# GpSimd waits for each slot's gathers to land before it begins the next slot's, in both layers of a two-layer graph network

## The reference

```python
h = relu(layernorm(x)); h0 = h @ W + b
agg = segment_sum(edge_weight[:, None] * h0[src], dst, 6250)
x = x + relu(agg / (segment_sum(edge_weight, dst, 6250)[:, None] + 1e-6))
h = relu(layernorm(x))
messages = gelu(concat([h[src], edge_attr]) @ W_msg + b_msg)
x = x + gelu(((1 + eps) * h + segment_sum(messages, dst, 6250)) @ W_upd + b_upd)
```

## Time and profile before

| | us |
|---|---|
| timed runs, median of 3 | 2670.86 |
| timed runs, lowest and highest | 2669.74, 2680.39 |
| profiled execution, span | 4082.0 |

### The profile page before, as it was taken

The page is one execution under the profiler, slowest core; times in us unless marked ns, Lnnn a source line. Parts: engine busy times, 40 slices in busy tenths (PEclk is TensorE's granted clock), DMA queues, the critical chain, the costliest instruction groups (busy, mean ns, idle before and its releaser), DMA issues.

```text
span 4082.0 us, 72599 instructions
## 1 busy us (share of the span) xinstructions
PE 2950.6 (72%) x22325; PEld 2600.4 (64%) x22326; DVE 2089.7 (51%) x4376; ACT 1607.4 (39%) x5144; POOL 1835.1 (45%) x1911
## 2 busy tenths in 40 slices
PE   2776766665665666576788788778878878878887
PEld 2666665554554555565677677677767767767777
DVE  8444445544544554544455455555545545555554
ACT  2343333433433443334344444444434444444443
POOL 2333344334434434424455545545545554554552
PEclk9888787877777777787888888888888888888888
DMA  4000000000000000002333333333333333333332
GB/s 92 14 12 14 13 16 16 13 13 15 14 12 15 15 13 14 15 14 66 75 84 85 81 81 84 87 79 83 88 76 86 83 81 81 84 87 78 85 88 52
DMA packets 473123, 214.39 MB, mean 53 GB/s; under 512 B 264996, under 2 KB 442024, under 8 KB 473076
## 3 DMA queue, kind: packets, MB, share of 16 engines
q1 hardware_dynamic: 412404, 151.55, 14.2%
q0 software_dynamic: 60672, 62.25, 9.2%
HBM read 208.14 MB, written 5.51 MB: 52 GB/s over the span
## 4 chain that ended last, share of the span: by engine, by line
PE 41%; issue 11%; another core or an unknown queue 1%; DVE 1%; DVEq 0%; ACT 0%; ACTq 0%
PE ps L918 28%; PE ps L1123 6%; PE ps L988 5%; PE ps L1112 2%; DVE sel L1451 0%; PE ps L1070 0%; DVE rows L1455 0%; DVEq L1464 0%; PE ps L1017 0%; ACT eT L844 0%; DVE sums_sb L1472 0%; DVE parts L1219 0%; DVE room L1654 0%; ACT dw L652 0%
## 5 line engine op out<-in xcount | busy, mean ns | idle before, releaser
L629 POOL DMA_INDIRECT rows<-p_table,idx x1176 | 1109.4, 943 | 1065.6 <-ACT idx L660 736.0
L918 PE MATMUL ps<-parts,pick_all 128*128 128x448 f32 x5488 | 1241.0, 379 | 63.5 <-issue 59.9
L629 POOL DMA_INDIRECT rows<-h_table,idx x720 | 709.5, 985 | 1062.1 <-ACT room L760 857.7
L918 PEld LDWEIGHTS ps<-parts,pick_all 128*128 128x128 f32 x5488 | 1046.3, 195 | 193.6 <-issue 109.4
L947 PE MATMUL ps<-adj,h_sb 128*64 128x160 f32 (+1 forms) x4802 | 503.4, 342 | 516.4 <-issue 469.9
L947 PEld LDWEIGHTS ps<-adj,h_sb 128*64 128x64 f32 x4802 | 404.4, 170 | 608.8 <-issue 551.9
L1451 DVE TENSOR_TENSOR sel<-ps,mask 128x896 f32<-128x896 f32 x196 | 213.5, 1089 | 761.4 <-remote 541.9
L1388 DVE TENSOR_SCALAR hot_p<-iota_p,scal 128x256 fp32r<-128x256 f32 (+1 forms) x848 | 309.4, 365 | 410.9 <-PE ps L928 321.6
L928 PE MATMUL ps<-hot_c,hot_p 128*128 128x125 f32 (+1 forms) x2336 | 456.3, 302 | 87.6 <-issue 72.4
L721 ACT COPY adj<-ps 128x500 f32<-128x500 f32 (+1 forms) x848 | 389.8, 524 | 203.0 <-PE ps L928 126.5
L928 PEld LDWEIGHTS ps<-hot_c,hot_p 128*128 128x128 f32 x2336 | 377.4, 207 | 110.5 <-issue 86.5
(11 more groups left out here) (181 smaller groups left out, 2975.9 us busy)
## 6 DMA issues: line engine op xcount, KB each, us to landing
src_all<-keys SPq DMA_DIRECT2D x196, 448.0 KB
ea<-in_edge_attr_dram SPq DMA_DIRECT2D x196, 256.0 KB
rows<-p_table,idx POOLq DMA_INDIRECT x1176
rows<-h_table,idx POOLq DMA_INDIRECT x720
x_sb<-in_x_dram SPq DMA_DIRECT2D x6, 224.0 KB, 3.5
h_table<-h_sb SPq DMA_DIRECT2D x6, 224.0 KB
p_table<-h_sb SPq DMA_DIRECT2D x6, 224.0 KB
out_dram<-h_sb SPq DMA_DIRECT2D x6, 224.0 KB
```

The source lines that it names most:

```text
L629: nc.gpsimd.indirect_dma_start(out=rows[:, s, j, 0:D], out_offset=None, in_=table[:, :], in_offset=bass.IndirectOffsetOnAxis(ap=idx[:, s, ...
L918: last = nc.tensor.matmul(to, hot[:, k, t * P:(t + 1) * P], parts[:, part, k, :, :].rearrange("p a d -> p (a d)"), start=(k == 0 and part ...
```

## The change

`gathers` gets a third argument, the level of the slot's semaphore at which this turn's gathers have all landed. After it has issued a slot's gathers, POOL waits for that level and only then goes on to the next slot. The last body of layer 1 is called without it. `s_passed` is a counter that nobody waits for. Nothing else changes.

```diff
-                def gathers(turn, tiles):
+                def gathers(turn, tiles, landed=None):
                     for s in range(SLOTS):
                         pool.wait_ge(s_const, CONSTS)
                         pool.wait_ge(s_idx[s], turn)
...
                         for j in tiles:
                             nc.gpsimd.indirect_dma_start(
...
                             ).then_inc(s_gat[s], 16)
+                        if landed is not None:
+                            pool.wait_ge(s_gat[s], landed)
+                            pool.sem_inc(s_passed, 1)
 
                 if layer == 0:
                     for z in ZONES:
                         with pool.Fori(z.first + 1, z.end + 1) as turn:
-                            gathers(turn, range(z.JA, J))
+                            gathers(turn, range(z.JA, J), z.gathered(turn - 1) * 16 + 16 * z.JH)
                 else:
                     with pool.Fori(BODIES + 1, 2 * BODIES) as turn:
-                        gathers(turn, range(J0))
+                        gathers(turn, range(J0), 16 * GATHERED + (turn - BODIES) * (16 * J0))
                     gathers(2 * BODIES, range(J0))
```

## The result

The changed kernel takes 3438.98 us (median of 4 runs, 3428.53 to 3445.61), the kernel before 2675.62 beside it: a ratio of 1.286, 95% interval 1.282 to 1.290. That is +763 us, where +600 were forecast; the time lies 9 us above the top of the range.

What follows compares the result with a forecast made beforehand. POOL's gather issue was taken as the bound, at its limit in layer 0 and nearly so in layer 1; bodies of 22.2, 27.2 and 37.8 us with start, transition and end summed to 3266, said as 3270 us (+22%), range 3076 to 3410.

Steps and rivals of the forecast that it cites:

- The page's 45% of POOL: Whole kernel: POOL is busy for 45% of the profiled span, which taken alone says a wait on it costs nothing.
- +1.8 us in layer 0: Each added wait in layer 0: landing 1.25 us, restart 0.77 and semaphore 0.1, in place of a 0.30 us gap.
- 1.95 in layer 1: Mean price in us of each added wait in layer 1, where SP's loads use the same DMA engines.
- 7.2: POOL's body in zones 0 and 1: the us a body that the added waits cost there.
- The sum for before: Unchanged kernel without PE's crawl: bodies of 15.0, 20.3 and 32.1 us and the rest sum to 2669, against median 2670.86.
- POOL is at its limit in layer 0, and 2 us a body short of it in layer 1: Timed runs before the change: POOL needs 15.0, 20.0 and 30.0 us of bodies of 15 to 17, 20.3 and 32.1.
- The crawl: PE's slow matmuls (nine in 16.60 us in L947), taken for the 1411 us that only the profiled execution has.
- a span of 4082 to 4810: Changed kernel's profiled execution: 4082 if POOL's idle time swallows the waits, 4810 if the crawl grows with POOL's burst.
- B: Rival: POOL has slack in timed runs too (45% busy, 17 us idle), so waits are hidden; time 2671; 5%.
- D: Rival: pauses free PE, which gets back more than POOL loses (trace offers 17.2 and 12.2 us); about 2515; 3%.
- C: Rival: without a profiler POOL issues a gather in 0.94 us in place of 1.25; time near 2790; 6%.
- The forecast's upper bound, 3410: Top of the range: waits at most +2.0 us in layer 0 and +2.5 in layer 1.

## Why the prediction was wrong in its size

**The mechanism stands.** The page's 45% of POOL is no slack: the added waits come end to end with the gathers on the engine that then sets the pace. Small loads, later waits and fewer waits each moved the time by what POOL's own sum says, once its gaps were known.

**The step that failed is the size of a wait**, "+1.8 us in layer 0" and 1.95 in layer 1; the runs show +2.05 for three waits of layer 0 and +2.5 for the one at the branch, and +2.3 in the mean of layer 1's four. The first reading that it rests on is how long a landing takes. In the changed kernel the gather of 903.43 to 904.37 (POOL's timeline above) has all its packets in 904.35:905.55, and lands 2.4 us after its issue:

```profile
q0 software_dynamic: 32, 0.03, 15.5%
...
rows<-h_table,idx POOLq DMA_INDIRECT x1, 2.4
```

The terms:
- Landing. The last packet's end was rightly read as 1.25 us, but the semaphore's way after it is not 0.1. In these lines the packets are done 1.2 us after the instruction's end and the landing is 1.5 after it, so the way is about 0.3. The page of after has 2.5 us from issue to landing over all gathers of layer 0, 0.94 of them the instruction, so 1.5 to 1.55. With a restart of 0.8 to 0.85 (0.77 forecast) this is the gap of 2.35, +2.05 a wait. The experiment with the wait one gather later fits this split: 1.24 us of a landing pass beside another gather, and layer 0's gap fell from 2.35 to 1.0. The Trainium skill ("DMA: Bandwidth & Descriptors", Anatomy of one DMA) has about 2.0 us fixed for such a transfer by GpSimd's way, most of it the receipt of the write. Counted from the instruction's end, with the same restart, that would have given 2.5 a wait, so the runs stand between my row and that figure; counted from the issue it is less than the 2.5 us measured.
- The loop's branch. The fourth wait stands ahead of it and its gap is 2.8, +2.5. The gather of the lines above is the one that it waits for, and lands no later than others (2.4 us against 2.5), so the 0.45 us more come after the landing. The order of instructions had shown it with the register work (`REGISTER_ALU [waits gathered3]`), and I gave it the price of the others.
- Layer 1. I spread SP's delay evenly at +0.15. It fell on two of four waits, 0.5 and 0.2 us, and depends on when SP's loads start beside the awaited gather: with two waits a body it was 1.7 us after slot 3 and 2.2 after slot 1.
- The gathers themselves. In layer 0 they take 984 ns in the mean, not 944. The page of before has this too (985, in a group that I didn't use for it). It is 0.04 x 16 = 0.7 us a body in zone 1, 0.3 in zone 0. The long ones go with DVE's work: from 500 to 1000 us of the changed kernel those that overlap its L1393 take 1.03 us in the mean and the others 0.95; no experiment took that work away. Rows 3 have one of 1.61 us beside the 1.59 that I took for the longest; the longest of the changed kernel is 1.54, and of any run 2.36 (one gather, with the waits in layer 0 alone).

In zone 1 this is 3 x 2.05 + 2.5 + 0.7 = 9.4 a body where 7.2 stood; the body of 29.6 us has 0.2 more. Zone 0's 24.0 us and layer 1's 39.3 are off by 1.8 and 1.5. Together 14.5 x 1.8 + 33 x 2.4 + 48 x 1.5 = 177 us. Two other terms were too high: body 1's slot 2 starts at 112 and not 118, and from the last weighting to layer 1's first gather are 48 us and not 61. That leaves 158, and the span of 3426.7 is 161 above the sum of 3266.

**The sum for before was right by luck**, 2669 with bodies of 15.0, 20.3 and 32.1 that are really 17.1, 21.3 and 30.5. So "POOL is at its limit in layer 0, and 2 us a body short of it in layer 1" was wrong in both halves: it is 1.9 and 1.1 us short of it in layer 0 and 0.6 in layer 1. Zone 0 had been set at POOL's need, the lowest it could be. Layer 1 came from two PE slots of which one had a part at a lower clock: its 28 matmuls took 6.63 us at a mean granted clock of 0.88, the others' 5.92 at 1.00. The forecast of after didn't suffer, since POOL's pace alone is in it; what I expected of each layer alone afterwards, +429 and +350, did.

**The crawl.** That it was of the profiled execution alone is right. That GpSimd's bursts bring it on (and so a span of 4082 to 4810) is wrong: the same kernel profiled once more has none, with the same bursts, and the changed kernel's span was 3426.7. What the crawl was stays open. The idle time that B rested on, and the 17 us that D offered, were both of that execution.

**The rivals.** B falls with the result; a wait is hidden where it fits (zone 0 with one wait), and 1.9 us of room was the most there was. C falls: an execution as fast as the timed ones shows 0.94 + 0.30 a gather. D falls: no kernel here was faster than before. The forecast's upper bound, 3410, allowed 8.0 us a body for the waits in layer 0, and it was 9.0 and 9.6 with the longer gathers; in layer 1 the 10.0 that it allowed were more than the 9.3 that came.

No version here beats the kernel before. The one that keeps its time, with waits for the slot before, gains nothing by them.

## What to carry to other kernels

An engine that issues DMAs back to back can be the bound at 54% busy, because the time between two issues counts; a wait for its own transfer there costs the whole landing and restart (2 us here and up to 4.3 beside other loads), and nothing measurable if it is asked one slot later. Before reading slack from a profile, see that its span agrees with the timed runs; where it doesn't, profile again before summing. When a sum meets the measured time, check its parts by another view: ours met it within 0.1% with each part wrong by 5 to 12%.

## What the runs showed of the hardware

A gather of 128 rows of 256 B lands 1.5 to 1.55 us after GpSimd's instruction ends, and a gather that waited for it starts 0.8 us after that, or 1.3 where the loop's branch stands between. With 704 KB of loads from another queue issued within a microsecond before it, the gap is 4.7 us, and 2.7 with the loads cut to 96 KB, though the gather is only 32 KB. TensorE's granted clock was 1.00 of full speed (2.4 GHz) in the three stretches shown of before in its second profile (busy for 586 of 661 us in zone 1), and 0.85 in the mean of zone 1 of the changed kernel, where it has more gaps (687 of 917 us); that cost nothing that the chain shows, which has 2% of PE.
